# A four-layer graph kernel: the SELU, residual and normalization after attention 1, moved into groups of four tiles on TensorE, ScalarE and VectorE

## The reference, cut to what matters

```python
def _L0_gnn_ref(...):                     # graph attention, 8 heads of 16
    alpha = exp(leaky_relu(a_src[src] + a_dst[dst]) - amax[dst])
    out = segment_sum(x[src] * alpha / asum[dst], dst) + bias
    return jax.nn.selu(out)
x = _layernorm(x + _L0_gnn_ref(x, ...))   # (v - mean) / sqrt(var + 1e-5)
x = _layernorm(x + _L1_gnn_ref(x, ...))   # x + sums over incoming edges, three times, with dense layers
x = _layernorm(x + _L2_gnn_ref(x, ...))   # graph attention, 4 heads
x = _layernorm(x + _L3_gnn_ref(x, ...))   # three graph convolutions with edge weights
```

## Time and profile before

| what | value |
|---|---|
| timed median of three runs | 6791.23 us |
| profiled execution, first to last instruction | 7088.1 us |
| profiled execution above the timed median | 296.9 us |
| SELU stage in the profile | about 1418 to 2513 us |
| GpSimd's scatters into the first plane, first to last start | 1369.6 to 2511.4 us |
| TensorE clock granted in the stage | 0.50 of full speed |

### The profile page before, as it was taken

The page is one execution under the profiler, slowest core; times in us unless marked ns, Lnnn a source line. Parts: engine busy times, 40 slices in busy tenths (PEclk is TensorE's granted clock), DMA queues, the critical chain, the costliest instruction groups (busy, mean ns, idle before and its releaser), DMA issues. The chain is left out here.

```text
span 7088.1 us, 38690 instructions
## 1 busy us (share of the span) xinstructions
PE 3209.9 (45%) x11661; PEld 2004.2 (28%) x11661; DVE 3016.5 (43%) x5694; ACT 1786.0 (25%) x1871; POOL 3469.4 (49%) x3338
## 2 busy tenths in 40 slices
PE   3000000000000079999999500000015999999999
PEld 2000000000000067777778400000013444544544
DVE  5565565555546723345667344444445000000111
ACT  1233333100000056666667322222210000000000
POOL 3677777677667755556767277777730000000000
PEclk8555555555555589999999755555557999999999
DMA  3365555208960056433358333333323888888887
GB/s 108 132 208 175 191 170 191 96 0 304 373 248 0 0 185 208 147 106 111 112 170 255 113 99 110 107 98 107 98 69 116 286 294 294 287 294 294 293 299 261
DMA packets 502441, 1242.14 MB, mean 175 GB/s; under 512 B 114227, under 2 KB 162841, under 8 KB 493273
## 3 DMA queue, kind: packets, MB, share of 16 engines
q1 hardware_dynamic: 382408, 1114.01, 46.0%
q0 software_dynamic: 119824, 125.65, 7.6%
HBM read 861.79 MB, written 377.50 MB: 175 GB/s over the span
## 5 line engine op out<-in xcount | busy, mean ns | idle before, releaser
L361 POOL DMA_INDIRECT gb<-rows,src x1564 | 1590.9, 1017 | 675.7 <-issue 545.9
L756 PE MATMUL psum<-gb,big 128*128 128x512 f32 (+1 forms) x3822 | 1579.3, 568 | 3.0 <-DVE gb L780 2.0
L595 POOL DMA_INDIRECT plane<-total,cell x782 | 846.6, 1083 | 543.9 <-DVE gb L576 187.5
L1110 ACT CAST strips<-gb 128x1024 fp32r<-128x1024 f16 (+1 forms) x764 | 805.9, 1077 | 1056.2 <-DMA gb<-plane 907.9
L1828 PE MATMUL psum<-identity,end_top 128*8 128x128 f32 (+1 forms) x2 | 0.7, 374 | 2278.1 <-issue 1173.8
L595 POOL DMA_INDIRECT plane<-begun,cell x782 | 819.3, 1048 | 323.8 <-issue 235.5
L1093 PE MATMUL psum<-strips,high 128*128 128x512 f32 (+1 forms) x1274 | 398.1, 400 | 1246.1 <-issue 1234.7
L756 PEld LDWEIGHTS psum<-gb,big 128*128 128x128 f32 x3822 | 691.5, 190 | 770.9 <-issue 770.9
L558 DVE SCALAR_TENSOR_TENSOR psum<-gb,psum 128x782 f32<-128x782 f32 (+31 forms) x782 | 490.3, 684 | 401.4 <-remote 235.6
L1828 PEld LDWEIGHTS psum<-identity,end_top 128*8 128x8 f32 (+1 forms) x2 | 0.2, 82 | 2278.8 <-issue 1174.2
L1812 ACT COPY gb<-turned 128x1632 f32<-128x1632 f32 (+3 forms) x138 | 450.6, 3266 | 727.8 <-DVE turned L1901 507.3
(11 more groups left out here) (305 smaller groups left out, 3776.8 us busy)
## 6 DMA issues: line engine op xcount, KB each, us to landing
gb<-plane SPq DMA_DIRECT2D x588, 512.0 KB, 4.4
gb<-plane SPq DMA_DIRECT2D x294, 576.0 KB, 4.8
plane<-turned SPq DMA_DIRECT2D x49, 3200.0 KB
gb<-plane SPq DMA_DIRECT2D x588, 256.0 KB
gb<-plane SPq DMA_DIRECT2D x294, 288.0 KB
plane<-turned SPq DMA_DIRECT2D x49, 1600.0 KB
runs<-gb SPq DMA_DIRECT2D x33, 1748.0 KB
runs<-gb SPq DMA_DIRECT2D x33, 1610.0 KB
```

The lines of the kernel that those rows point to most:

```text
L361: m.s_rows[b % BUFS].up(nc.gpsimd.indirect_dma_start(m.batch(b, columns, row)[:, j, 0:width], None, table, bass.IndirectOffsetOnAxis(ap=m. ...
L595: done.up(m.nc.gpsimd.indirect_dma_start(plane, bass.IndirectOffsetOnAxis(ap=m.cell[:, r:r + 1], axis=0), total[:, r:r + 1], None), 16)
L756: mm = nc.tensor.matmul(m.psum[:, self.bank(r, 0, i), 0:nodes], rows, slot[:, a:a + nodes], start=(s == 0), stop=False)
L1110: m.s_strip_act.up(nc.scalar.copy(out, landed))
```

## The change

1. The SELU stage becomes a class `Selu`. VectorE only divides, by groups of four tiles, with the reciprocal now in PSUM (bank 5). Per group TensorE adds the bias in PSUM (identity matmul and ones matmul, bank 6), ScalarE makes relu(-v), 1.0507 * relu(v) and the exponential, TensorE sums x, both parts and a constant in bank 7, ScalarE copies the sum to x.
2. The normalization is by groups too: BN_STATS and BN_AGGR on VectorE, root on ScalarE, reciprocal and shift on VectorE, then ScalarE applies scale and shift tile by tile into PSUM (bank 6 or 7), rounds and copies; VectorE subtracts for `low_part` from PSUM.
3. VectorE counts one group of columns between two groups of tiles. `degrees` (the `dinv` part) comes after g7 and waits for a root of ScalarE, which stands behind all 13 joined groups.
4. The wipe is issued at the stage's begin, and the store of x behind it.
5. `unread` becomes one stretch of PSUM and one of SBUF, which frees banks 5 to 7.

```diff
-        self.unread = [flat[:, n * 1024:n * 1024 + COLS] for n in (2, 3)]
+        self.unread = [flat[:, 2 * COLS:3 * COLS], self.junk[1]]
...
+    def divide(self, dve, c):
+        c.link(nc.vector.tensor_scalar(z, sums[:, :, :, D // H], SOFTMAX_EPS, None, ALU.add))
+        c.link(nc.vector.reciprocal(self.inverse, z))
+        for g in range(QUADS):
+            m.s_divided.up(nc.vector.tensor_tensor(self.out[:, t, :]..., sums[:, t, :, 0:D // H], self.inverse[:, t, :]..., ALU.mult))
+    def pe(self, pe):
+        self.add_bias(pe, 0)                   # two matmuls of 512 columns
+        for g in range(QUADS):
+            if g + 1 < QUADS:
+                self.add_bias(pe, g + 1)
+            self.join(pe, g)                   # four matmuls of 512 columns
+    def act(self, act):
+        for g in range(QUADS):
+            ...                                # Relu, Relu, Exp of 512 columns
+            if g:
+                self.keep_joined(act, g - 1)   # copy of 512 columns
+        self.keep_joined(act, QUADS - 1)
+        act.wait_ge(m.s_degree.sem, m.s_degree.at(1))
+        m.s_act_turn.up(nc.scalar.activation(m.var[:, :], m.var[:, :], ACT.Sqrt))
+        for g in range(QUADS):
+            self.normal(act, g)                # root, one Identity per tile, two copies
+    def dve(self, dve):
+        count_edges(m, dve, COUNTED_BEFORE, COUNTED_AHEAD)
+        self.divide(dve, c)
+        for k, b in enumerate(groups):         # g7 to g33
+            count_edges(m, dve, b, b + 1)
+            if k == 0:
+                self.degrees(dve, c)
+            elif k <= QUADS:
+                self.statistics(dve, c, k - 1)
+            if 2 <= k <= QUADS + 1:
+                self.split(dve, k - 2)
...
-            sp.wait_ge(m.s_out.sem, m.s_out.at(1))
-            m.s_kept.up(sp.dma_start(by_tile(m.kept), x), 16)
             wipe(m, sp, 1, 0, TILES)
+            sp.wait_ge(m.s_normal_kept.sem, m.s_normal_kept.at(QUADS))
+            m.s_kept.up(sp.dma_start(by_tile(m.kept), selu.x), 16)
```

More of the change, by code:

```diff
@@ L1 @@
 from contextlib import ExitStack
+import math
 import concourse.bass as bass
@@ L210, in __init__ @@
         self.step = flat[:, 0:2 * COLS]
-        self.unread = [flat[:, n * 1024:n * 1024 + COLS] for n in (2, 3)]
+        self.unread = [flat[:, 2 * COLS:3 * COLS], self.junk[1]]
+        assert 3 * COLS <= 5 * 512
         self.signals = []
@@ L305, in __init__ @@
         self.s_shifted = signal("s_shifted")
+        self.s_divided = signal("s_divided")
+        self.s_biased_sum = signal("s_biased_sum")
+        self.s_below = signal("s_below")
+        self.s_above = signal("s_above")
+        self.s_exp = signal("s_exp")
+        self.s_joined = signal("s_joined")
+        self.s_joined_kept = signal("s_joined_kept")
+        self.s_var = signal("s_var")
+        self.s_root = signal("s_root")
+        self.s_stats = signal("s_stats")
+        self.s_normal = signal("s_normal")
+        self.s_normal_kept = signal("s_normal_kept")
+        self.s_rounded = signal("s_rounded")
+        self.s_degree = signal("s_degree")
     def next_pass(self):
@@ L2016, in selu_stage @@
 def selu_stage(m, own, bias):
[L2019 to L2022, removed]
+    selu = Selu(m, own, 8, bias)
+    with m.nc.Block(no_gpsimd_drain=True) as block:
         @block.vector
         def _(dve):
[L2026 to L2045, removed]
@@ L2047, in _ @@
+            selu.dve(dve)
         @block.scalar
         def _(act):
[L2049 to L2056, removed]
@@ L2057, in _ @@
-            m.s_parts.up(nc.scalar.copy(m.high[:, :, :], rounded))
+            selu.act(act)
+        @block.tensor
+        def _(pe):
+            selu.pe(pe)
         @block.sync
         def _(sp):
-            sp.wait_ge(m.s_out.sem, m.s_out.at(1))
-            m.s_kept.up(sp.dma_start(by_tile(m.kept), x), 16)
             wipe(m, sp, 1, 0, TILES)
+            sp.wait_ge(m.s_normal_kept.sem, m.s_normal_kept.at(QUADS))
+            m.s_kept.up(sp.dma_start(by_tile(m.kept), selu.x), 16)
         @block.gpsimd
```

117 lines of the change are left out of this document (added).

## The result

The changed kernel takes 6733.31 us (median of 4 runs, 6729.21 to 6735.2); the kernel before, run beside it on the same chip, 6792.06 (6787.08 to 6793.98). The ratio is 0.9914, with a 95% interval of 0.9902 to 0.9926: 58.7 us faster, 50 to 67 by the interval. Forecast were 6737 us and 54.0 less.

The account below looks back on a forecast made before the run. GpSimd's scatters were taken to bound the SELU stage, TensorE the stage after. 54.0 us of stretched scatters come off GpSimd's line, nothing is added: 6791.2 - 54.0 = 6737.2 us, range 6698 to 6783.

Parts of the forecast that it names:

- The lock-out: SELU stage: VectorE's whole-array passes stretch nine GpSimd scatters; removing them takes 54.0 us off GpSimd's line, bounds 28 to 54.0.
- What is late next is GpSimd itself.: SELU stage after the change: GpSimd's scatters, at their usual cadence, still end last, so the 54.0 us count in full.
- 2.33 us holds: VectorE's counts in the SELU stage held by something the profile doesn't name: 235.6 us in 108 waits.
- the prediction's own sign of being wrong: Wrong if scatters stay stretched, waits for VectorE's counts grow by the lock-out's gain, or timed gain is below 28 us.
- Hunger, 88 us: SELU stage: GpSimd waits 88.0 us in 9 waits for VectorE's late counts of column groups; forecast to stay near 88.
- rival B: SELU stage: VectorE's freed time also ends GpSimd's waits for counts, so all 142 us go: 6649 us; chance 0.07.
- TensorE and ScalarE, 5.3 us a group: Six fp32 matmuls and ScalarE's work per group of four tiles: 13 groups take 69 us (43 to 73), beside GpSimd's scatters.
- g8, 6 us late or 60 sooner: Column group counted after the stand for `degrees`: about 6 us late for GpSimd as recorded, 60 earlier without VectorE's earlier holds.
- Statistics, 20 us: SELU normalization: 49 BN_STATS and 49 BN_AGGR on VectorE at 0.2 us each, 20 us (14 to 38), hidden between counts.
- C: SELU stage: some small divides, splits or BN_STATS block scatters too, so only 28 us gained, 6763 us; chance 0.08.
- D: Slower: VectorE's stand for `degrees` delays g8; at 12 us a group 39 us slower, 6830 us; chance 0.05.
- A: VectorE's held counts set GpSimd's pace in timed runs too, so 35 us gained (8 to 37), 6756 us; chance 0.20.

Follow-up runs that it names:

- squares: Kernel before plus eight whole-array TENSOR_TENSORs (x times x, two SBUF inputs) on VectorE behind the normalization: 6840.74 us, ratio 1.0064.
- scalings: Kernel before plus sixteen whole-array TENSOR_SCALARs (one SBUF input) on VectorE behind the normalization: 6836.88 us, ratio 1.0065.
- reductions: Kernel before plus eight whole-array TENSOR_REDUCEs (one SBUF input) on VectorE behind the normalization: 6799.62 us, ratio 1.0002.

## Why the prediction was right, and where it was not

**The lock-out, 54.0 us.** Right, in mechanism and size. The nine long scatters held 54.6 us over their 0.97, and all of them are gone; squares, scalings and reductions behave as read from the earlier trace rows. The rest of the 58.7 us is 2.3 on the scatters' line, nearly all of it the 3 ns of each, and 1.8 outside it, which the interval doesn't resolve. The lower bound has a slip: divides, splits and half the statistics are 27.2 us and not 26, which moves nothing.

**"What is late next is GpSimd itself."** Right where the kernel before takes some 6800 us: no wait for a count in 782 scatters. But the ground I gave was wrong in kind. I took the 2.33 us holds for something that recording adds. The new recording of before adds nothing (span 6797.6, timed median 6798.21). The holds belong to a condition of the machine, seen on one chip and in the first recording, in which timed runs take 7100 us too. Where it holds, the change gains nothing: it took 4.4 us more, with an interval that takes in no difference. There the prediction's own sign of being wrong came true, that the waits for counts grow by what the lock-out gave. That the timed runs of before had no such holds I had read rightly from their shorter time; that the changed kernel was then timed where they are absent is luck, for on the other chip the same change gains nothing. The rule that I applied, to carry the gain in microseconds from a recording 4.4% long to the median, gave the right number because the scatters' busy time is the same in both conditions to 0.1 us; the stage's waits are not.

**Hunger, 88 us, and rival B.** There was none to take in the timed runs. B could not come true in either condition: in the one there is no wait, in the other the changed kernel waits more (149.9 us) than before.

**TensorE and ScalarE, 5.3 us a group.** Mis-sized. An fp32 matmul of 512 columns takes 0.86 to 1.05 us from start to start at the full clock and 1.7 to 2.0 at half, where I took 0.43 and 0.86. The "x4" in 1.72 us are entries of the trace, and one fp32 matmul makes two of them. That is the misreading. So six matmuls are 5.9 us warm, TensorE and not ScalarE sets the group's pace (busy 40.00 of the 40 us from 1410 to 1450; 6.6 us a group measured, with the cold begin), its chain lasts 86.2 us where 45 to 75 were given, and the stand is 71.8 us, not 53. Nothing of this error showed in the time, for the counts behind the stand still come 48.8 us early.
The Trainium skill (FP8 and Floating Point Precision, "TensorE Precision Notes") says that a true fp32 matmul goes through the array in four passes; with one column a cycle, four passes of 512 columns at 2.4 GHz would be 0.85 us, an estimate from that page, and the trace's 0.86 behind equal weights agrees.

**g8, 6 us late or 60 sooner.** Measured 48.8 us early where the kernel before takes 6800 us, and 47.4 late where it takes 7100. The first lies near my guess for a run without holds (54 early). In the second g7 is counted at 1598.2 us and not at 1564, because its counts are held some 34 us in all, and the stand is 12 us longer than I put it; I had counted only the holds of the recording before.

**The clock.** 1.2 GHz (0.50) for the first 13 us of the burst, then mostly 2.4 GHz (0.96 from 1410 to 1450 us): the rise that I left open came. It fell back to 0.50 three times for 3.4 us, first from 1406.6 to 1410.0 us, although TensorE had been busy without a pause since 1396; a matmul took 1.71 us in it again. The rows name no cause for these falls.

**Statistics, 20 us.** 49 BN_STATS in 10.7 us and 49 BN_AGGR in 4.7, 15.4 in all, inside the bounds. A split takes 0.68 us where I had 0.66; the divides follow each other every 0.57. All of it is hidden.

**The wipe and `unread`.** Nothing, as said. The wipe ends at 1765.9, some 80 us before the time I gave because the whole stage begins 78 us earlier than in the first recording. The accumulator is read in 0.080 us for the output in SBUF and in 0.138 for that in PSUM, but the counts follow each other at the same pace with either (0.375 us for 230 columns), so of the 0 to 0.1 us given it is 0.

**The rivals.** C is excluded: behind the first six scatters none is above 1.2 us, so no divide, split or BN_STATS blocks. D works as described, but begins to cost at some 10.4 us a group and not at 5.3. A's mechanism and the forecast are both true, each in its condition, and the recording on which I built was one of A's; A's price of 35 us is right in neither.

## What to carry to other kernels

When GpSimd issues indirect DMAs all through a stage, price VectorE's work there by its operands. Here a whole-array pass with two SBUF inputs took some four fifths of its length from GpSimd, and so did plain scalings, which go at twice the rate. Reductions and passes with one input in PSUM took nothing as long as GpSimd had work queued, and thirteen passes of 0.57 us with two SBUF inputs took 1.9 us together. When the profiled execution is several per cent longer than the timed one, treat it as another condition of the machine and record again before using its waits; here the scatters' busy time carried over to 0.1 us and the waits did not, nor did the gathers' busy time (954 and 1017 ns each). And before a matmul's cost is read off a row, see how many entries the trace has for one instruction of the kernel: an fp32 matmul stands as two here.

## What the runs showed of the hardware that was not expected

The 7100 us condition. On that chip the kernel before took 7089 to 7109 us in every run, on the others 6787 to 6803. The last layers, which are TensorE's, take 1675.6 to 1675.7 us in both. What grows is where engines hand over to each other often: the gathers of one attention layer from 1087 to 1166 us (mean 954 to 1017 ns each), the scatters' waits, the strips from 1419 to 1452. The trace says "remote" or "issue" for the holds on VectorE and names no cause. That it goes with the chip rather than with the hour was not tried, and what makes it stays open.

A blocked GpSimd is let through once between two blocking passes even when they follow each other without a gap: one scatter per 6.69 us pass, eight times in eight, and one per two passes of 3.43 us. Its row lasts from its begin inside one pass to shortly after the begin of a later one (6.42 and 6.62 us).
